# Expert weights loaded as pairs of pieces, 1 MB a transfer instead of 512 KB

## The reference, cut to what matters

```python
x = x + _L0_xattn_ref(_layernorm(x), ...)
x = x + _L0_attn_ref(_layernorm(x), ...)
x = x + _L0_ffn_ref(_layernorm(x), ...)
# in _L0_ffn_ref, HIDDEN = 1024, MOE_INTER = 512, N_EXPERTS = 16, TOP_K = 2
topk_indices, topk_weights = _router(x, router_weight, e_bias)
combine = zeros((T, N_EXPERTS)).at[arange(T)[:, None], topk_indices].add(topk_weights)
h1 = einsum('th,ehi->tei', x, w_up)
a = relu2(h1) * combine[:, :, None]
routed = einsum('tei,eih->th', a, w_down)
shared = relu2(hidden_states @ shared_up) @ shared_down
return routed + shared
```

## Time and profile before

| | |
|---|---|
| median of 3 runs | 1428.79 us (1427.3 to 1429.11) |
| the profiled execution, its own time | 1429.72 us |
| span of the profiled execution | 1427.8 us |
| granted TensorE clock, mean | 0.998 |
| busy: PE, PEld, DVE, ACT, POOL | 98%, 80%, 60%, 37%, 13% |
| DMA over the whole span | 203.63 MB, mean 143 GB/s |
| packets of all DMA queues | 43485 |

### The profile page before, as it was taken

The page is one execution under the profiler, slowest core; times in us unless marked ns, Lnnn a source line. Parts: engine busy times, 40 slices in busy tenths (PEclk is TensorE's granted clock), DMA queues, the critical chain, the costliest instruction groups (busy, mean ns, idle before and its releaser), DMA issues. The chain is left out here.

```text
span 1427.8 us, 18180 instructions
## 1 busy us (share of the span) xinstructions
PE 1402.1 (98%) x6676; PEld 1147.2 (80%) x6676; DVE 849.8 (60%) x1236; ACT 530.4 (37%) x951; POOL 191.5 (13%) x264
## 2 busy tenths in 40 slices
PE   7999999999999999999999999999999999999998
PEld 5878888888888888888888888867777788888887
DVE  5654455555554555555445547576877676687665
ACT  3222322233222223322222322555643435676561
POOL 3000100000000000000000000253432013112022
PEclk9999999999999999999999999999999999999999
DMA  7454653333333333333333231400110456988765
GB/s 251 156 192 150 233 179 123 111 118 110 110 112 123 125 110 117 111 110 112 123 125 110 89 126 67 148 1 1 60 34 1 161 168 212 323 304 291 263 239 206
DMA packets 43485, 203.63 MB, mean 143 GB/s; under 512 B 5232, under 2 KB 5296, under 8 KB 31984
## 3 DMA queue, kind: packets, MB, share of 16 engines
q1 hardware_dynamic: 29152, 149.17, 29.9%
q0 software_dynamic: 9568, 36.35, 8.0%
q10 hardware_dynamic: 4704, 17.30, 3.1%
HBM read 182.36 MB, written 20.45 MB: 142 GB/s over the span
## 5 line engine op out<-in xcount | busy, mean ns | idle before, releaser
L32 PE MATMUL banks<-V_hi,b_PT_hi 128*128 128x512 f32 x512 | 205.5, 401 | 0.0
L1035 ACT ACTIVATE b_PT_hi<-banks 128x512 fp32r<-128x512 f32 x64 | 38.3, 599 | 447.1 <-PE banks L766 447.1
L34 PE MATMUL banks<-V_hi,b_PT_lo 128*128 128x512 f32 x512 | 200.1, 391 | 0.0
L33 PE MATMUL banks<-V_lo,b_PT_hi 128*128 128x512 f32 x512 | 199.6, 390 | 0.0
L34 PE MATMUL banks<-K_hi,QT_lo 128*128 128x512 f32 x512 | 199.4, 389 | 0.0
L32 PE MATMUL banks<-K_hi,QT_hi 128*128 128x512 f32 x512 | 199.3, 389 | 0.0
L33 PE MATMUL banks<-K_lo,QT_hi 128*128 128x512 f32 x512 | 199.2, 389 | 0.0
L1275 DVE TENSOR_TENSOR b_scores<-banks,b_scores 128x512 f32<-128x512 f32 x64 | 44.2, 691 | 199.4 <-PE banks L34 199.4
L649 POOL DMA_DIRECT2D b_scores<-mask x60 | 32.2, 537 | 638.5 <-PE banks L766 626.4
L2218 DVE TENSOR_TENSOR e_lo<-e_raw,e_hi 128x1024 fp32r<-128x1024 f32 x80 | 96.8, 1252 | 33.2 <-ACT e_hi L2043 32.6
L34 PEld LDWEIGHTS banks<-V_hi,b_PT_lo 128*128 128x128 f32 x512 | 96.1, 188 | 21.0
(11 more groups left out here) (329 smaller groups left out, 2737.3 us busy)
## 6 DMA issues: line engine op xcount, KB each, us to landing
raw<-kv SPq DMA_DIRECT2D x60, 1024.0 KB, 4.7
e_raw<-w_up SPq DMA_DIRECT2D x40, 512.0 KB, 5.6
e_raw<-w_down SPq DMA_DIRECT2D x40, 512.0 KB, 6.0
b_scores<-mask POOLq DMA_DIRECT2D x64, 256.0 KB, 2.9
d_s_raw<-shared_w SPq DMA_DIRECT2D x26, 512.0 KB, 4.4
raw<-xattn_w SPq DMA_DIRECT2D x11, 1024.0 KB, 4.8
y_dram<-c_zeros ACTq DMA_DIRECT2D x1, 6656.0 KB, 26.8
raw<-attn_w SPq DMA_DIRECT2D x6, 1024.0 KB, 4.8
```

The lines of the kernel that those rows point to most:

```text
L32: pe.matmul(out, lhs_hi, rhs_hi, start=first, stop=False)
L33: pe.matmul(out, lhs_hi, rhs_lo, start=False, stop=False)
L34: return pe.matmul(out, lhs_lo, rhs_hi, start=False, stop=last)
L1035: act.activation(PT_hi[:, u % 2, :], T_ps[:, u % 2, :], ACT.Copy).then_inc(b["pt_hi"], 1)
```

## The change

A load now brings two pieces, k and k+1, in one transfer of 1 MB into two neighbouring slots. SP waits until both pieces that lay there have been split (one piece later than the first of them had to wait for), two of the four landing semaphores are gone, and ACT waits for the pair's semaphore before either piece. Nothing else changes: the slots, the ring, the order on each engine, and what ACT, DVE and PE do with a piece. 80 transfers become 40.

```diff
-        e_loaded0 e_loaded1 e_loaded2 e_loaded3 e_hi e_split e_used sp_waited
+        e_loaded0 e_loaded2 e_hi e_split e_used sp_waited
...
             def load_expert(k, j, what, e):
 
                 if not isinstance(k, int) or k >= EXPERT_RAW:
-                    sp.wait_ge(s["e_split"], k - EXPERT_RAW + 1)
+                    sp.wait_ge(s["e_split"], k - EXPERT_RAW + 2)
                     sp.sem_inc(s["sp_waited"], 1)
-                src = ins["w_up"][e][:, 2 * j:2 * j + 2, :] if what == "up" else ins["w_down"][e][:, j, :]
-                dst = wide(e_raw[:, j, :]) if what == "up" else e_raw[:, j, :]
+                src = ins["w_up"][e][:, 2 * j:2 * j + 4, :] if what == "up" else ins["w_down"][e][:, j:j + 2, :]
+                dst = e_raw[:, j:j + 2, :]
+                if what == "up":
+                    dst = dst.rearrange("p a (e n) -> p (a e) n", n=W)
                 sp.dma_start(dst, src).then_inc(s[f"e_loaded{j}"], 16)
...
             def load_chunk_up(c, k):
                 e = expert_of(c)
-                for j in range(4):
+                for j in range(0, 4, 2):
                     load_expert(k + j, j, "up", e)
 
             def load_chunk_down(c, k):
                 e = expert_of(c)
-                for j in range(4):
+                for j in range(0, 4, 2):
                     load_expert(k + j, j, "down", e)
...
             def expert_hi(k, turn, j, first):
 
-                act.wait_ge(s[f"e_loaded{j}"], turn * 16)
+                act.wait_ge(s[f"e_loaded{j - j % 2}"], turn * 16)
```

## The result

The kernel with pairs takes 1437.94 us (1434.81 to 1445.32 over eight runs), the kernel before 1429.07 us (1427.17 to 1431.31) on the same chip. The ratio is 1.0066, with a 95% interval of 1.0052 to 1.0080: it is slower, by about 9.4 us (7.4 to 11.4); the two medians lie 8.9 apart. The forecast was 1433.9 within 1429 to 1442.

A forecast was written before the change was run, and what follows sets the result against it. PE, busy 98% with 0.7 us of waits, bounds the kernel; late landings at four places cost 2.1 + 0.9 + 1.1 + 1.0 = 5.1 us, moving the span from 1427.8 to 1432.9 and giving a median of 1433.9 us, range 1429 to 1442.

The forecast's parts named there:

- the turn of the loop: Pair of slots, wait to split: 8.3 us a turn with nothing in the way, against 8.82 us available from PE.
- Removed issues: On SP: 40 fewer DMA issues and two fewer semaphores, claimed worth nothing, since SP only waits and issues.
- Packets: DMA packets fall from 43485 by 5120 + 640 if packets are of 8 KB, by 640 alone if not.
- The timing of chunk 1: Pair 18/19 lands 1.1 us late; with the extra ACT step a_hi(1) is 2.1 late, down(1) loses 2.1 us.
- Chunk 2: At down(2): two turns take 18.5 us against PE's 17.64, less 0.28 to spare; 0.9 us lost, ends 0 and 2.5.
- Chunk 3: At down(3), 20.45 us after down(2): PE's other work covers it, 0 us lost, up to 1.
- Four places with under 0.4 us to spare: Before down(1), down(2), down(8) and at shared_lo(23): spare 0.06, 0.28, 0.37 us, and an existing 0.5 us wait.
- Piece 51: At shared_lo(23), near 1312 us: rounding moves by 0.96, shared_lo(23) by 1.1; 1.1 us lost, ends -0.5 and 2.2.
- Chunk 8: At down(8), pair 74/75: 0.96 extra step, about 0.4 later start, less 0.37 to spare; 1.0 us, ends 0 and 2.
- The sum: Whole expert stage: 2.1 + 0.9 + 1.1 + 1.0 = 5.1 us lost; low ends 0.5, high ends 11.4.
- The larger transfer paying for itself: Rival, crowded expert-stage loads: pairs land early enough to pay the ACT step; 1428.1 to 1431 us, chance 0.22.
- That the loop limits the whole stage: Rival, expert stage: turns of 9.3 to 9.6 us, 10 us lost, 1439, at most 1443; chance 0.19.

The follow-up runs named there:

- e3: Changed kernel with both waits kept, but each pair sent as two 512 KB transfers on one semaphore: 1439.11 us, ratio 1.0068.
- e12: Changed kernel once more, unchanged, for a second profile and more runs: 1437.58 us, ratio 1.0066.
- e1: Kernel before, single 512 KB transfers, but a pair's first piece is issued only when both slots have been split: 1431.31 us, ratio 1.0026.
- e8: Changed kernel with the store of y for chunks 0 to 6 cut from 1024 to 128 columns: 1430.28 us, ratio 1.0012.
- e6: Changed kernel, but ACT and DVE treat only the first 512 of a piece's 1024 columns: 1429.12 us, ratio 1.0006.
- e7: Changed kernel with its waits, but each pair's transfer carries only its first piece, 512 KB: 1428.06 us, ratio 0.9998.
- e9: Only the w_up pieces paired, w_down pieces single as in the kernel before: 1428.20 us, ratio 0.9995.
- e11: Changed kernel with the gather of each chunk's rows cut from 1024 to 128 columns: 1435.15 us, ratio 1.0040.
- e2: Kernel before, loads issued as before, but ACT uses neither piece of a pair until both have landed: 1433.98 us, ratio 1.0044.
- e10: Only the w_down pieces paired, w_up pieces single as in the kernel before: 1436.07 us, ratio 1.0049.
- e5: Kernel before with a_hi, a_lo of chunks 1 to 3 and shared piece 23's steps moved ahead of the last two down pieces: 1428.61 us, ratio 1.0000.
- e4: Changed kernel with a_hi, a_lo of chunks 1 to 3 and shared piece 23's steps moved ahead of the last down pair: 1436.42 us, ratio 1.0055.

## Why the prediction was right, and where its sizes were off

The direction, the mechanism and the range held: slower, through a late landing that reaches PE at small steps behind the pieces. The forecast of 1433.9 was 4.0 us short of the median; the term that was too small is the turn of the loop, by the landing of a down pair.

**Removed issues, worth nothing.** Nothing contradicts it: e3 issues 80 transfers, after 40, and they take the same time within the 3 us that can be told.

**Packets.** Forecast 43485 - 5120 - 640 = 37725, found 37723. The transfer is what it says.

**The timing of chunk 1.** SP's timeline and ACT's, at the pairs 14/15 and 18/19:

```profile
1216.39 4.96 SPq L1728 DMA_DIRECT2D e_raw<-w_down  x2
```

```profile
1217.33 2.01 ACT L2045 ACTIVATE e_hi<-e_raw 128x1024 fp32r<-128x1024 f32 x2 [2.66 <-DMA e_raw<-w_up]
...
1223.80 2.01 ACT L2045 ACTIVATE e_hi<-e_raw 128x1024 fp32r<-128x1024 f32 x2 [3.37 <-DMA e_raw<-w_down]
...
1228.80 2.01 ACT L2045 ACTIVATE e_hi<-e_raw 128x1024 fp32r<-128x1024 f32 x2 [2.98 <-DMA e_raw<-w_down]
1230.71 0.58 ACT L2061 ACTIVATE e_aT_hi<-banks 128x512 fp32r<-128x512 f32 x1
```

Pair 14/15 was there at 1217.3 (forecast 1217.0). Pair 18/19 was issued at 1216.39 + 4.96 - 0.33 = 1221.0 (1220.7) and there at 1228.8 (1228.2). The two ACT steps stand together, and `a_hi(1)` behind them. From up(0) to down(1) 2.05 us were lost in the first profile and 1.8 in e12, so the 2.1 was right as a number. Its parts, 1.1 for a later landing and 0.96 for the ACT step, are not shown: e1 has no such step and loses 2.25, and e3, with the waits of after, loses 4.8 in its one profile. In part the size was luck.

**Chunk 2, and the turn of the loop.** This is the term that was mis-sized. I had 18.5 us for two turns (two of 8.3 are 16.6, not 16.7) against PE's 17.64, and so 0.9 for chunk 2 and nothing for chunk 3. The splits of pieces 18/19 and of 34/35, two chunks apart, are in DVE's timeline of after:

```profile
1229.89 2.36 DVE L2220 TENSOR_TENSOR e_lo<-e_raw,e_hi 128x1024 fp32r<-128x1024 f32 x2 [2.63 <-ACT e_hi L2045]
...
1270.58 2.36 DVE L2220 TENSOR_TENSOR e_lo<-e_raw,e_hi 128x1024 fp32r<-128x1024 f32 x2 [2.10 <-ACT e_hi L2045]
```

That is 40.69 us, or 20.3 for each chunk, and 19.8 in e12. Before, from piece 19 (split at 1229.42) to piece 35 (1262.53), it was 33.11 us, or 16.6 for each chunk, less than PE's 17.64. The lines of before:

```profile
1228.19 1.23 DVE L2218 TENSOR_TENSOR e_lo<-e_raw,e_hi 128x1024 fp32r<-128x1024 f32 x1 [0.29 <-ACT e_hi L2043]
...
1260.18 2.35 DVE L2218 TENSOR_TENSOR e_lo<-e_raw,e_hi 128x1024 fp32r<-128x1024 f32 x2
```

The same stretch, piece 19 to piece 35, in one profile of each run, goes roughly with what the run loses. PE needs 17.64 us for the first of these two chunks and 20.45 for the second. In e8, 1.4 us of the loss stand at chunk 8 and not here.

| run | piece 19 to 35, us | against before, us |
|---|---|---|
| e6 | 33.5 | +0.9 |
| e8 | 35.8 | +1.7 |
| e7, e9 | 36.5, 36.5 | -0.3, -0.7 |
| e1 | 37.5 | +3.7 |
| e11, e2 | 38.0, 38.1 | +5.7, +6.3 |
| e10 | 39.0 | +7.0 |
| e12, after | 39.6, 40.7 | +9.4 |
| e3 | 41.0 | +9.7 |

What had the wrong size was the landing of a down pair: 4.7 in light traffic and 0.9 for the store make 5.6, and it took 7.4. For pair 18/19 I had myself taken 7.5, from piece 19, and did not carry it into the loop. The up pairs, at 5.1, were near. With 0.2 us of waiting, 2.0 for ACT and 1.4 for DVE in each turn, 5.1 and 7.4 give 8.7 + 11.0 = 19.7. I had priced the store at half of what its bytes are worth; e8 shows that it adds 2.4 us to a down pair's landing. Chunk 2 so cost 2.7 us in the first profile (1.1 waited, 1.5 at the lower clock), and in e12 1.45 at down(2) and then 1.35 at the shared unit before down(3).

**Chunk 3, nothing.** Down(3) itself has no wait, as forecast. But the margin was smaller than I wrote: the 2.8 us are PE's 20.45 less its 17.64, and against my 18.5 for two turns it is 1.95. And `shared_lo(16)`, which stands between the pieces of down(3), was not among my places, nor a shared unit behind down(3), where PE waits 0.44 us (1285.54, after) and 0.64 (1283.65, e12). Before, `shared_lo(16)` had 3.1 us to spare, by DVE's timeline and PEld's:

```profile
1259.04 1.22 DVE L2197 TENSOR_TENSOR d_s_lo<-d_s_raw,d_s_hi 128x1024 fp32r<-128x1024 f32 x1
```

```profile
1263.39 0.19 PEld L32 LDWEIGHTS banks<-d_xT_hi,d_s_hi 128*128 128x128 f32 x1
```

Four places with under 0.4 us to spare were the right list for a small delay and too short a list for one that grows. Counted from up(0), pieces 19, 27 and 35 are split 2.0, 5.0 and 9.6 us later than before. After that the delay shrinks (piece 51: 6.6), since PE takes 109.92 us from down(3) to down(8), 22 for each chunk and longer than the loop.

**Piece 51.** 1.9 us at shared 23 in the first profile, of which 2.18 - 0.53 = 1.65 is the wait, and 1.52 - 0.53 = 1.0 in e12 (its wait there is 1.52); forecast 1.1, with an end at 2.2.

**Chunk 8.** 1.0 forecast. None in the first profile (0.0), where the sum of what was lost before is as large as in e12 with it, and 1.25 in e12, 1.40 in e8. PE that is later needs less there: the places are not independent, and adding them up is right only as long as each is small.

**The sum.** 5.1 us forecast, 7.4 and 7.5 in the two profiles from up(0) to the end, 8.9 between the medians and 9.4 by the ratio. The first 2.3 are the loop. The remaining 1.5 to 2 are not in that stretch of the two profiled executions. In part that is the choice of executions: the profiled one of before took 0.65 us more than its median and that of e12 1.5 less than its own. Stretches at the lower clock are not their cause: the two executions of after whose mean granted clock is 1.000 take 1436.7 us, and those of before with 1.000 take 1426.5 to 1428.0, so the difference is as large among them. More likely the waits vary: the runs of after scatter over 10.5 us where those of before scatter over 4, and e3, with the waits of after, shows 13.4 us of PEld's waits in the one execution that was profiled, its slowest (1443.95 us):

```profile
PEld banks L32 <- DVE e_aT_lo L2231: 8.3, 3, 3.8
PEld banks L32 <- issue: 2.7, 3, 1.3
PEld banks L32 <- DVE d_s_lo L2198: 2.4, 1, 2.4
```

What makes a landing late in one execution and not in the next stays open.

**The rivals.** The larger transfer paying for itself is out: e3 is the test of it. e3 with 512 KB takes 1439.11 and after with 1 MB 1437.94, which these runs can't tell apart. The prediction had set beside this rival the rule of the Trainium skill, "DMA: Bandwidth & Descriptors", Bandwidth, to batch to at least 1 MiB. It did not bear on the time here. The page gives it with the rate of transfers by their size; that it counts a queue that is always fed was my remark and not the page's. That the loop limits the whole stage was given 0.19 and more than 1437. It was nearer than the 0.19 said: its time (1439) and its chunk of the loop, 18.6 to 19.2 (measured 19.8 and 20.3), fit better than mine. But the loop does not limit the whole stage. Of 7.4 us, 4.7 are lost by down(3), 1.9 from there to shared 23 and 0.8 behind down(8). The waits that were to be its sign, for the pieces themselves at up(c) or at every chunk, did not come; the waits stayed at the small steps.

**No kernel here beats the one before.** e5 and e9 equal it, as they must with 0.7 us of waits to win. A third pair of slots would have loosened the loop; it was not tried, since the kernel leaves about 3 KB of on-chip memory free in each partition and a pair of slots needs 8.

## What to carry to other kernels

Where few buffers go round in a loop (wait for the buffer free, load, convert, free it again), work out the length of a turn against the consumer's time for it, stretch by stretch, before making transfers larger: merging two loads adds the first one's wait, the second one's landing and a conversion step to each turn, and saves only an issue. Price a store or a gather that meets such a load by what it does to the load's landing in a trace, not by its bytes. Where the loop is longer than the consumer's time, moving the step at which the wait shows only moves the wait.

## What the runs showed of the hardware that was not expected

A store of 512 KB beside 1 MB loads put their landing from 5.0 to 7.4 us (e8 against e12), though the store's bytes at the rates of the earlier trace rows are worth at most 1.9.

After a wait of PE in a stage where it is otherwise always busy, the granted clock fell to 1.2 GHz for 3.5 to 5 us in some cases and not in others. It fell behind waits of 2.32 us (after), 4.65 (e4) and, some 2 us later, 3.12 (e3); it stayed at 2.4 GHz behind waits of 2.09 (e12), 2.40 (e1), 2.18 (after, at 1319.57) and 3.8 (e3, near 1236). The length of the wait alone does not decide it here. By an estimate it costs 1.5 to 2.4 us when it comes: 7 weight loads fewer in 3.5 us of after than in the same stretch of e12, and 11 fewer in the 5 us of e4 at e12's rate, at 0.22 us each. By the two profiles of the kernel with pairs, nothing of it is added where PE would have waited for the loop anyway.
